# A gated cross-attention block: loading x and its transpose batch by batch, weights of the last product last

## The reference

```python
# attention over the context; the "values" are the layer-normed x itself
query = ctx @ Wq.T + bq;  key = ctx @ Wk.T + bk          # 4 x 256 x 128
attention = softmax(query @ key.T, axis=-1)              # 4 x 256 x 256
x_m = layernorm(x) @ attention.T                         # "bln,bmn->blm"
x = x + tanh(g_xattn) * x_m
# feed-forward: 256 -> 2 x 1024 -> 256, operands rounded to fp8 (e4m3)
h = layernorm(x)
act = gelu(h @ w_gating[0]) * (h @ w_gating[1])
x = x + tanh(g_ffn) * (act @ w_linear)                   # w_linear: 1024 x 256
```

## Time and profile before

| | |
|---|---|
| time, median of 3 runs | 56.52 us (56.35 to 56.79) |
| span of the profiled execution | 54.7 us |
| busy: PE, PEld | 43.6 us (80%), 28.7 us (53%) |
| busy: DVE, ACT, POOL | 39.6 us (72%), 29.6 us (54%), 30.7 us (56%) |
| granted TensorE clock, mean | 0.993 |
| loads | 16 DMA engines about full from 2.5 to 19 us, then nearly idle until the stores |

### The profile page before, as it was taken

One profiled execution on the slowest core, in us unless ns is written; L12 is line 12 of the kernel. 1 busy time (PEld: TensorE's weight loads), 2 busy tenths in 40 slices (PEclk: granted clock), 3 DMA queues, 4 the chain that ended last, 5 costly groups with the idle time before them and its releaser, 6 DMA issues.

```text
span 54.7 us, 874 instructions
## 1 busy us (share of the span) xinstructions
PE 43.6 (80%) x245; PEld 28.7 (53%) x245; DVE 39.6 (72%) x113; ACT 29.6 (54%) x67; POOL 30.7 (56%) x57
## 2 busy tenths in 40 slices
PE   1999999919999401998289999999999999998200
PEld 0338888707888101983234364664564668884000
DVE  1110099999960059998999999949998599889930
ACT  4413636597897930633148966697444693555000
POOL 4109700079992009889898889888884079302200
PEclk9999999999999999999999999999999999999997
DMA  0597999999999700000000000000000003520063
GB/s 0 142 296 175 361 337 263 192 201 204 196 200 279 310 9 0 0 0 0 6 0 0 0 12 0 6 0 0 0 6 0 0 0 113 181 102 0 0 252 131
DMA packets 3461, 5.43 MB, mean 99 GB/s; under 512 B 384, under 2 KB 1792, under 8 KB 3456
## 3 DMA queue, kind: packets, MB, share of 16 engines
q1 hardware_dynamic: 2880, 4.85, 27.0%
q0 software_dynamic: 576, 0.52, 10.3%
HBM read 5.90 MB, written 1.05 MB: 127 GB/s over the span
## 4 chain that ended last, share of the span: by engine, by line
PE 36%; DMA 23%; DVE 13%; SPq 11%; issue 5%; ACT 5%; POOL 1%; DVEq 1%; ACTq 0%
DMA wl<-w_linear 23%; PE bank L686 12%; PE bank L711 11%; PE bank L692 11%; SPq L227 5%; SPq L219 3%; DVE x L483 3%; DVE aq L527 3%; DVE st L488 2%; SPq L217 2%; ACT gl L397 2%; DVE xh L502 2%; PE bank L668 2%; POOL r L274 1%; ACT ys L405 1%
## 5 line engine op out<-in xcount | busy, mean ns | idle before, releaser
L397 ACT ACTIVATE gl<-bank 128x512 bf16<-128x512 f32 (+1 forms) x20 | 10.0, 509 | 6.4 <-PE bank L686 6.4
L518 DVE SCALAR_TENSOR_TENSOR ap<-bank,gl 128x512 f16<-128x512 f32 (+1 forms) x20 | 11.5, 577 | 2.2 <-PE bank L692 1.5
L711 PE MATMUL bank<-wl_q,aq 128*128 128x256 bf16 x64 | 10.1, 273 | 0.8 <-DVE aq L527 0.6
L686 PE MATMUL bank<-xq,wg 128*128 128x512 fp8e4 (+1 forms) x40 | 10.2, 337 | 0.2 <-ACT xq L388 0.2
L692 PE MATMUL bank<-xq,wg 128*128 128x512 fp8e4 (+1 forms) x40 | 10.2, 337 | 0.0
L527 DVE TENSOR_SCALAR aq<-ap 128x512 uint16<-128x512 uint16 (+1 forms) x20 | 8.5, 430 | 0.0
L711 PEld LDWEIGHTS bank<-wl_q,aq 128*128 128x128 f16 x64 | 5.8, 97 | 4.7 <-DVE aq L527 2.3
L646 PE MATMUL bank<-attnT,xT_sb 128*128 128x256 f32 x32 | 8.1, 385 | 0.0
L302 POOL TENSOR_TENSOR wl_sum<-wl_big,wl 128x256 f32<-128x256 f32 x8 | 5.9, 734 | 0.5
L618 PE MATMUL bank<-ident,attn 128*128 128x128 f32 x16 | 2.5, 280 | 4.5 <-POOL attn L283 3.3
L307 POOL TENSOR_TENSOR wl_q<-wl_sum,wl_big 128x256 bf16<-128x256 f32 x8 | 5.8, 728 | 0.5
(11 more groups left out here) (54 smaller groups left out, 69.8 us busy)
## 6 DMA issues: line engine op xcount, KB each, us to landing
x_sb<-x SPq DMA_DIRECT2D x4, 256.0 KB, 5.0
wl<-w_linear SPq DMA_DIRECT2D x2, 512.0 KB, 10.0
xT_sb<-xT SPq DMA_DIRECT2D x4, 256.0 KB, 11.0
out<-yo SPq DMA_DIRECT2D x6, 128.0 KB, 1.9
wg<-w_gating POOLq DMA_DIRECT2D x4, 128.0 KB, 10.1
par<-params_ctxT SPq DMA_DIRECT2D x1, 258.0 KB, 2.7
par<-params_ctxT SPq DMA_DIRECT2D x1, 256.0 KB, 4.5
out<-yo SPq DMA_DIRECT2D x1, 256.0 KB, 2.0
```

The lines of the kernel that those rows point to most:

```text
L397: nc.scalar.activation(gl[:, s % 2, toks], gate_b[s % 2][:, toks], ACT.Gelu_apprx_tanh).then_inc(gelu_ready, 1)
L518: nc.vector.scalar_tensor_tensor(ap[:, s % NAP, toks], up_b[s % 2][:, toks], ACT_SCALE, gl[:, s % 2, toks], ALU.mult, ALU.mult).then_inc(p ...
L686: mm = nc.tensor.matmul(gate_b[s % 2][:, toks], wg8[:, c, k, 0, o:o + P], xq[:, g, k, toks], start=(k == 0), stop=(k == KC - 1))
L711: mm = nc.tensor.matmul(halves(y_b[g][i])[:, t], aq[:, s % NAQ, m:m + P], wl_q[:, j], start=(j == 0 and t == 0), stop=(j == HT - 1), skip_ ...
```

## The change

Three orders change, and nothing that is computed. On SP, the loads of x and of its transpose alternate by batch, and both halves of w_linear come last. On DVE, the first statistics of batches 1, 2 and 3 stand between the softmax steps instead of ahead of them, and the exponents of the weights' two halves move from within the softmax to behind `norm2(0)` and `norm2(1)`. On POOL, the normalising of batch 3 moves between the two shifts, and the rounding of weight block 0 moves behind `rstd2(0)` and `rstd2(1)`.

```diff
@@ sync
             for b in range(B):
                 sp.dma_start(x_sb[:, b], x[b]).then_inc(s_x[b], 16)
-
-            def load_w_linear(h):
+                sp.dma_start(xT_sb[:, b], xT[b]).then_inc(s_xT[b], 16)
+            for h in range(2):
                 half = slice(h * HT // 2, (h + 1) * HT // 2)
                 sp.dma_start(wl32[:, half], w_linear[:, half]).then_inc(s_wl[h], 16)
-
-            load_w_linear(0)
-            for b in range(B):
-                sp.dma_start(xT_sb[:, b], xT[b]).then_inc(s_xT[b], 16)
-            load_w_linear(1)
@@ gpsimd
             scales1()
             shift_x(0)
+            normalise(B - 1)
             shift_x(1)
+            rstd2(0)
+            rstd2(1)
             wl_constant(0)
-            normalise(B - 1)
             wl_up(0)
-            rstd2(0)
             wl_down(0)
             wl_constant(1)
-            rstd2(1)
             wl_up(1)
             wl_down(1)
             round_wl(2)
@@ vector
-            for b in range(B - 1):
-                stats1(b)
+            stats1(0)
             row_max(0)
-            stats1(B - 1)
+            stats1(1)
             row_max(1)
             normalise(0)
-            wl_exponents(0)
+            stats1(2)
             row_max(2)
             normalise(1)
             row_max(3)
+            stats1(B - 1)
             normalise(2)
-            wl_exponents(1)
             invert_sum(B - 1)
             for b in range(2):
                 add_attention(b)
...
             norm2(0)
+            wl_exponents(0)
             norm2(1)
+            wl_exponents(1)
             add_attention(2)
```

## The result

The changed kernel takes 59.43 us (median of four executions) against 56.51. The forecast was 59.0, +2.5. The four took 59.93, 59.76, 59.10 and 58.96 us, at a mean granted TensorE clock of 0.941, 0.941, 0.970 and 0.991.

The account below looks back on a forecast made before the run. It took DVE's 3.8 us wait for w_linear and POOL's rounding, just on PE's path, as the bound. Later rounding adds 2.5 to the 54.7 span, 57.2, plus 1.8 from span to median: 59.0 us, range 57.5 to 60.1.

Parts of the forecast that it names:

- x of batch 3 at 14.65, by turns of the two queues packet by packet, not 13.7 by bytes: SP's load queue: x of batch 3, now seventh 256 KB, lands at 14.65 us instead of 8.8.
- Rival 1: SP's queue: x of batch 3 lands by bytes at 13.7, everything 0.95 earlier; 58.1 us, chance 0.20.
- DVE free at 13.3, so a wait of 1.35 us for x: DVE ahead of batch 3's first statistics: 6.4 us of work from 6.84, then waiting for x until 14.65.
- First addition at 20.05, behind a wait for POOL: DVE's first addition of attention waits for POOL's layer-norm shift: 20.05 instead of 20.46, 0.4 us gained.
- First constant at 25.2, last rounding at 44.2: POOL's weight rounding cannot begin before the exponents at 25.2; last block ends at 44.2 against 41.67, +2.5 us.
- The price of DVE against POOL: POOL's first round beside norm2(1) and second exponents on DVE: blocking between 0 and +0.9 us, taken as 0.
- Feed-forward from 26.9: PE's feed-forward starts at 26.9 instead of 28.08, a head start of 1.2 us, as norm2(1) ends near 25.7.
- Both paths say +2.5, they do not add: Eighth output product on PE: ready at 44.1 through ACT and PE, at 44.35 through POOL's rounding; only the later counts.
- PE's 9.9 us from the first gelu behind the standstill to the eighth product: PE needs 9.9 us from that gelu's end at 34.2 to the eighth output product, giving 44.1.
- Rival 4: Start of the feed-forward, not POOL's rounding, sets the end, so the removed stall comes through: -1.2, 55.3 us, chance 0.06.
- Rival 5: No difference: the shift at the eighth product is partly made good behind it; 56.5 us, chance 0.07.
- Rival 2: DVE and POOL blocking adds up, in the first round and at roundings of products: +0.9, 59.9 us, chance 0.16.

Follow-up runs that it names:

- e9: Changed kernel with POOL's four w_gating loads issued only once x of batch 3 has landed: 58.07 us, ratio 1.024 to the kernel before.
- e1: Changed kernel with SP loading x of all four batches first, then the transposes, then w_linear: 58.05 us, ratio 1.031 to the kernel before.
- e5: Kernel before with the change's exponent places on DVE and its POOL order, loads and statistics as before: 56.27 us, ratio 0.992.
- e2: Changed kernel with rstd2 of batch 2 ahead of the rounding of block 2 on POOL: 58.85 us, ratio 1.043 to the kernel before.
- e3: Changed kernel with the rounding of w_linear left out, one POOL instruction per block instead of three: 55.71 us, ratio 0.988 to the kernel before.
- e4: Kernel before with only the exponents of the second half of w_linear moved, behind norm2 of batch 1: 53.23 us, ratio 0.943.
- e7: Changed kernel with eight idle matmuls on PE ahead of the turn of batch 2's rows: 59.24 us, ratio 1.046 to the kernel before.
- e6: Kernel before with the change's statistics places and second-half exponents behind norm2 of batch 1, loads as before: 58.26 us, ratio 1.028.

## Why the prediction was right

By its own steps:

- *x of batch 3 at 14.65, by turns of the two queues packet by packet, not 13.7 by bytes.* It landed at 14.38. e9 shows that the other queue is the cause, and the counts of 72 and 77 packets that the turns go by packets. Rival 1's 13.7 was not met.
- *DVE free at 13.3, so a wait of 1.35 us for x.* DVE was free at 14.06 and waited 0.35. Most of the difference is waits for x of batches 0 and 1 that the estimate left out (a start at 7.00 instead of 6.84, then 0.47). With x in time (e1, e9) these statistics start at 13.7, not 13.3. So DVE's own order holds them back nearly as long as the load does, and "a late load of x takes the place of the late load of weights" is half of the cause. The forecast's time did not suffer, because it goes by the later of the two, and that was still the load. Rival 1's price for a start at 13.7, 58.1 us, is what e1 and e9 took (58.05 and 58.07).
- *First addition at 20.05, behind a wait for POOL.* 19.75; the 3.6 us wait is there.
- *First constant at 25.2, last rounding at 44.2.* 24.97 and 44.23. The two are right with two errors in between that cancel, and so far the closeness is luck. The price of DVE against POOL was taken as 0; it was +0.52: from the first constant to the third it took 29.71 - 24.97 = 4.74 instead of 4.22, because the first `wl_q` (1.26 instead of 0.73) stood until the second exponents on DVE, at 26.25, were done. e5 has the same pair of rows (1.26 on POOL at 23.12, beside the exponents at 23.12). The wait fell on POOL. "SBUF — State Buffer" of the Trainium skill (SBUF: two separate sides) has the two engines' shared port pair as an exclusive lock to whoever starts first; the trace agrees in that one instruction is held for 0.53 us while the other runs for 0.68, though the two rows start at the same time and do not show who was first. The forecast's sum had taken the other side. What made up for it: x was 0.27 earlier, and the last six rounds took 14.52, not 14.79.
- *Feed-forward from 26.9.* 27.47: `norm2(1)` ended at 26.32, not 25.7, blocked for the same reason. The forecast's head start of 1.2 us was 0.6. That cost nothing, as the start of the feed-forward is not on the path.
- *Both paths say +2.5, they do not add.* e2 bears it out at full clock. In the profiled execution it failed: the eighth product stood right behind its neighbour with POOL done 1.01 us before, which is one of the forecast's own signs of being wrong. The path over ACT and PE, forecast to be ready at 44.1, was ready at 45.24.
- *PE's 9.9 us from the first gelu behind the standstill to the eighth product.* This is the term that was mis-sized; it was taken from rows at full clock, and the sum had none for the clock. The path was right up to its start: the gelus began at 33.69 (forecast 33.6), though ACT waited 3.1 us for the shift of batch 2 (forecast about 4) and PE stood for 1.60 us (forecast two to three). From there PE took 10.95 us (45.24 less 34.29, the end of that gelu), with the clock at 0.50 from 35 to 38.5. In e1, at full clock there, the same stretch is 9.9 (33.6 to 43.5, when PE could have gone on). That put 0.9 us on the path (45.24 against 44.37).
- *The time.* The execution of 59.76 us had the same mean clock as the profiled one, 0.941; those with 0.970 and 0.991 took 59.10 and 58.96, near the forecast's 59.0. So the clock fits both the 0.4 us by which the median is above the forecast and the 1 us between the executions. That it is this in each of them is not shown, as only one has its trace; and why the clock fell there and not in e1 and e9 stays open.
- *Rival 4 (the stall comes through, 55.3 us)* is what e3 gives (55.7) with the rounding left out: the mechanism was right, its condition was not met. *Rival 5* is out by the constant tail. *Rival 2* gave blocking 0.9 us; on POOL's first rounds it was 0.52.

The order of the parts was not forecast. From e4 to the changed kernel it is 6 us: the change holds one move that is worth 3.2 us and surrounds it with others (the loads, the statistics, the exponents of half 0 with POOL's order) that together cost 6.0.

## What to carry to other kernels

Before you move work into a stretch, ask what idle time it leaves: POOL's first two rounds cost nothing ahead of 26.88 us, where the third began; placed behind 25 us, they put the third at 29.71, and the last rounding went with it (44.23 instead of 41.67). A wait that tops the list is worth removing by the smallest edit that does so; here one moved line gave 5.7%, and the wider reordering around it turned that into a loss of 4.9%. Where one instruction needs all batches at once (the scales of the first layer norm), the last batch's load and statistics are the first thing to place, not the last.

## What the runs showed of the hardware

- Two DMA queues moved nearly equal numbers of packets: 72 and 77 in the same microsecond, with 0.06 and 0.14 MB. A queue that alone moves 0.40 MB in 1 us (e9) falls to a third beside a casting load whose packets are small.
- A wait between DVE and POOL shows for tiny operands too: the power of a 128x2 tile on POOL took 1.20 us at 23.68 instead of 0.73, ending (24.88) when the exponents on DVE did (24.16 + 0.69). e2 and e5 have the same 1.20 with the same coincidence; the cause is inferred from it. Beside the exponents, POOL's constant of a block took 0.93 us in e4 (at 23.07) instead of 0.41.
- TensorE's granted clock fell to 0.50 in the changed kernel from 21 to 25 us and from 35 to 38.5. Before the first, PE had stood for 2.07 us; before the second, for 1.60 and in further short pauses. The length of a gap by itself does not tell: behind gaps of 2.07 to 2.09 us the clock fell in e1, e3, e7 and e9 and not in e2; behind 1.59 to 1.60 us it did not fall in e1, e5 and e9; before the change it did not fall behind 3.26 us; in e6 it fell while PE still stood, in a gap of 3.59 us. Where PE was held up anyway, as at 21 to 25, half the clock cost nothing: from the first addition to the feed-forward it is 7.72 us in the changed kernel (27.47 - 19.75) and 7.72 in e2 (28.63 - 20.91), which was at full clock.
